# One ring of six PSUM banks for score tiles and all other products of three attentions

## The reference

```
xn = layernorm(x)
s  = attention_L(xn)          # L = 0, 1, 3: causal softmax attention; L = 2: linear attention over 64 x 64 maps
g  = silu(ffn_L(xn))          # L = 0, 3: mixture of 8 experts; L = 1: 8 experts and a shared one; L = 2: dense
x  = x + s * g
```

```
logits = q @ k^T (scaled), positions after the query masked
w      = softmax(logits)
out    = concat_heads(w @ v) @ Wo
```

## Time and profile before

| | us |
|---|---|
| median of 3 runs | 1986.79 |
| lowest, highest | 1980.47, 1986.86 |
| span of the profiled execution | 1987.3 |
| TensorE busy | 1839.8 (93%) |
| VectorE busy | 1337.9 (67%) |
| GpSimd busy | 1239.5 (62%) |
| ScalarE busy | 963.6 (48%) |

### The profile page before, as it was taken

How to read it: one execution, slowest core, us unless ns; L and a number is a source line. 1 busy time by engine, 2 the same in 40 slices (tenths; PEclk the granted TensorE clock), 3 DMA queues, 4 the chain that set the end, 5 groups by cost and what they waited for, 6 DMA issues and landing times.

```text
span 1987.3 us, 31683 instructions
## 1 busy us (share of the span) xinstructions
PE 1839.8 (93%) x9960; PEld 1273.0 (64%) x9960; DVE 1337.9 (67%) x3765; ACT 963.6 (48%) x2008; POOL 1239.5 (62%) x1454
## 2 busy tenths in 40 slices
PE   5999999999895899999999999999889999998985
PEld 4566666666595566676766567887556666555564
DVE  8888888888344767666666546556776777764533
ACT  2534445445455455554555534545344545444543
POOL 1767789889654467767777710011367888799953
PEclk8999999999998899999999999999799999999997
DMA  5224243232153443443444220000313223223243
GB/s 150 67 61 116 64 107 91 63 78 61 53 175 85 95 95 82 109 95 90 102 93 100 66 88 22 1 13 1 85 44 71 63 69 77 69 67 86 63 122 101
DMA packets 138508, 155.95 MB, mean 78 GB/s; under 512 B 34420, under 2 KB 78740, under 8 KB 138084
## 3 DMA queue, kind: packets, MB, share of 16 engines
q1 hardware_dynamic: 134244, 145.80, 30.0%
q0 software_dynamic: 4096, 8.12, 1.2%
HBM read 47.96 MB, written 17.52 MB: 33 GB/s over the span
## 4 chain that ended last, share of the span: by engine, by line
PE 62%; DVE 12%; POOL 11%; issue 6%; DMA 3%; ACT 3%; SPq 2%; POOLq 0%; DVEq 0%; ACTq 0%
PE P L904 61%; POOL acc L1701 4%; POOL yd L1724 3%; DVE mx L2112 2%; DMA qA<-hq 2%; POOL acc L1698 1%; SPq L1828 1%; DVE P L2123 1%; POOL xg L1715 1%; POOL pr L1679 1%; PE P L1003 1%; ACT pr L1444 1%; PE P L942 0%; DMA xl<-yd 0%; POOL z L1707 0%
## 5 line engine op out<-in xcount | busy, mean ns | idle before, releaser
L1701 POOL TENSOR_TENSOR acc<-acc,pr 128x512 f32<-128x512 f32 (+5 forms) x640 | 660.3, 1051 | 47.2 <-ACT pr L1444 22.5
L1444 ACT ACTIVATE pr<-P 128x512 f32<-128x512 f32 (+1 forms) x768 | 396.7, 568 | 321.4 <-PE P L904 278.8
L904 PE MATMUL P<-pr,vt 128*64 128x512 f32 (+3 forms) x2304 | 402.7, 490 | 4.9 <-POOL pr L1679 4.9
L904 PE MATMUL P<-qA,kA 128*128 128x512 f32 (+2 forms) x1024 | 389.2, 383 | 12.5 <-ACT pr L1444 11.6
L904 PE MATMUL P<-qB,kB 128*128 128x512 f32 (+2 forms) x1024 | 367.7, 365 | 0.0
L904 PE MATMUL P<-kA,qA 128*128 128x512 f32 (+2 forms) x1152 | 314.8, 376 | 32.0 <-DMA qA<-hq 12.3
L1679 POOL TENSOR_SCALAR_AFFINE_SELECT pr<-pr 128x256 f32<-128x256 f32 x384 | 157.3, 411 | 275.6 <-ACT pr L1444 214.6
L904 PEld LDWEIGHTS P<-pr,vt 128*64 128x64 f32 x2304 | 154.0, 137 | 225.7 <-issue 191.1
L2112 DVE TENSOR_REDUCE mx<-P 128x1 f32<-128x512 f32 x384 | 243.4, 683 | 40.2 <-PE P L904 37.9
L904 PEld LDWEIGHTS P<-qA,kA 128*128 128x128 f32 x1024 | 195.1, 191 | 95.7 <-ACT pr L1444 46.6
L904 PEld LDWEIGHTS P<-kA,qA 128*128 128x128 f32 x1152 | 194.5, 197 | 94.7 <-issue 25.0
(11 more groups left out here) (355 smaller groups left out, 2847.4 us busy)
## 6 DMA issues: line engine op xcount, KB each, us to landing
qA<-hq SPq DMA_DIRECT2D x384, 128.0 KB
kA<-stage SPq DMA_DIRECT2D x158, 128.0 KB
qB<-qB SPq DMA_DIRECT2D x96, 128.0 KB, 2.3
kB<-stage SPq DMA_DIRECT2D x79, 128.0 KB
rb<-sum_share SPq DMA_DIRECT2D x60, 128.0 KB
yd<-in_c_zero SPq DMA_DIRECT2D x32, 128.0 KB, 2.7
w<-in_L_W SPq DMA_DIRECT2D x16, 256.0 KB
xg<-xg SPq DMA_DIRECT2D x24, 129.0 KB
```

The costliest lines, as they stand in the source:

```text
L904: return P.matmul(out, lhs, rhs, start=start, stop=stop)
L1444: S.activation(a.pr[slot][:, r, 512 - wide:512], m.bank[b][:, 512 - wide:512], AF.Exp, scale=0.125).then_inc(s.free[b], 1)
L1701: G.tensor_tensor(acc[:, :, sl], acc[:, :, sl], pt[:, :, sl], ALU.add).then_inc(s.acc, 1)
```

## The change

The scores' own ring is gone. Score tiles take their banks from aux, which now has six banks in the order 4, 5, 6, 2, 0, 1. In layer 3's table one step, k0', moves behind q0'; it is done once, in the eighth job, where the keys of the second block are projected. And the identity products before the last output are left out where they would write into the bank that the output product itself uses.

```diff
-         "score": ("score", 2), "pv0": ("pv", 1), "close": ("aux", 1), "out": ("aux", 1), "nbias": ("aux", 1),
+         "score": ("aux", 2), "pv0": ("pv", 1), "close": ("aux", 1), "out": ("aux", 1), "nbias": ("aux", 1),
...
-POOLS = {"aux": (4, 5, 6, 2), "score": (0, 1), "pv": (3, 7), "misc": (3, 7), "up": (0, 1, 2, 3), "dn": (4, 5), "tr": (6, 7),
+POOLS = {"aux": (4, 5, 6, 2, 0, 1), "pv": (3, 7), "misc": (3, 7), "up": (0, 1, 2, 3), "dn": (4, 5), "tr": (6, 7),
...
-    3: ("q0 + k0' + k0 k1 q0' k0\" S V3 + R1 S q0\" + v0 C1 S S + M1 M0 F1 k1' S q1' q1 S + + W1 Z1 q1\" M2 I1 + "
+    3: ("q0 + + k0 k1 q0' k0' k0\" S V3 + R1 S q0\" + v0 C1 S S + M1 M0 F1 k1' S q1' q1 S + + W1 Z1 q1\" M2 I1 + "
...
-                    if pair == p and k[1:] == (1, 7, 1):
+                    if pair == p and k[1:] == (1, 7, 1) and od.bank[IDLE_OUT[L][1]][0][0] != b:
                         idle(*IDLE_OUT[L])
```

## The result

The changed kernel takes 1988.32 us in the median of 20 runs (1981.33 to 1996.48), the one before 1985.40 in 20 runs beside them (1979.64 to 1990.63). The ratio of changed to before is 1.0021, 95% interval 1.0011 to 1.0031: 2 to 6 us slower, under the 0.5% named before the run. The forecast of 1991.3 us was 3 us too high, 1.4 us of it because it started from the median of three runs (1986.79). The +4.5 us of its sum stands against +4.1 us by the ratio and +2.9 by the medians.

A forecast was written before the change was run, and what follows sets the result against it. TensorE was taken to bound the attentions, GpSimd 1743 to 1905 us. Terms -1.0 + 6.3 - 2.1 + 1.0 + 0.7 + 0 - 0.4 = +4.5 us on 1987.3, less 0.5, gave 1991.3 us; range 1975 to 2003.

The forecast's parts named there:

- The first attention: 80 to 535 us: +6.3 us net; eleven query-bank waits (ten at M2, one at a score) +7.1, maxima's banks +2.9, gains -3.7.
- The 14 scores behind a maximum's reader: First attention: 14 score tiles take a bank a maximum just used, mean 0.2 us each, together 2.9 us lost.
- The start: 0 to 80 us: key projection starts 2.0 us sooner in a free bank; 1.0 us taken as gained.
- The second attention: Net -2.1 us: 1.6 lost at 14 scores behind maxima; first maxima 1.0, last job's tiles and small waits 2.7 gained.
- Before the third attention: First key projection waits for L2493 to free the last gated product's bank: +1.0 us; then +0.7 up to 1743 us.
- GpSimd's stretch: 1743 to 1905 us: TensorE gets 1.6 us back, but GpSimd is full, so 0 on the path.
- R2: Rival, slower: GpSimd runs dry from 1743 us, idle above 15 us; 2002.2 or 1999 us; 0.21 with other such losses.
- The end: Last output product: nine warming matmuls fall away, 0.4 us gained.
- The upper bound of +1.1 us: Last output product: if TensorE's clock falls to 1.2 GHz after the rest, its 1.06 us doubles.
- R1: Rival, faster: more banks lift the score waits wholesale, 23 us less 7.1, giving 1971 us; chance 0.13.
- R3: Rival, no effect: the query bank is free in time, 7.1 us falls away, 1984 us; chance 0.20 shared with R4.
- R4: Rival: the ring is wider but each wait only changes its name, 1987 us; chance 0.20 shared with R3.

The follow-up runs named there:

- e1: Ring of six in layer 0 alone, layers 1 and 3 as in the kernel before: 1990.44 us against 1986.13 for the kernel before, ratio 1.0021.
- e4: Kernel before with its two rings, but layer 0's maximum M2 takes the query bank let go last: 1989.69 us against 1986.13, ratio 1.0016.
- e3: Changed kernel, but a held bank goes to the ring's end when let go: 1980.53 us against 1986.13 for the kernel before, ratio 0.9961.
- e2: Ring of six in layers 1 and 3 alone, layer 0 as in the kernel before: 1986.51 us, ratio 0.9990 to the kernel before.

## Why the prediction was right

**The first attention, +6.3 us forecast.** Right in place and sign. The mechanism was there as told: M2 right behind L2084, 0.67 us late at 367 us. But it wasn't the same in every job. Taking the excess over 0.23 us at M2 for the maxima of the third to the sixteenth job (85.77 to 486.07 us), the changed trace has 0.67 or 0.68 eight times, 0.58 and 0.59 once each, 0.16 once and nothing three times: ten jobs with a full wait, as counted, and 6.7 us in all, close to the 7.1. The waits between 170 and 505 us, changed kernel:

```profile
PE P L904 <- DVE qB L2084: 4.3, 9, 0.5
...
PEld P L904 <- DVE mx L2123: 3.8, 14, 0.4
...
PEld P L904 <- DVE qB L2084: 0.9, 1, 0.9
```

The one load wait of 0.9 us is the score that meets a query's bank (at 184.59), the forecast's eleventh place.

The 14 scores behind a maximum's reader are there too, 14 times as counted, with a mean of 3.8 / 14 = 0.27 us at the load. At the place of the earlier trace rows, 281.82 us in the changed kernel, the load waits 0.23 us for L2123, where the forecast had 0.29. So the two losses stand nearly as counted. The eleven jobs show +3.74 us, but they are 326 of the forecast's 455 us. From 58.67 to 118.03 us (57.64 to 118.87 in the changed kernel, M2 of the first and of the third job) it is +1.87, and from 118 to 177 us the two traces can't be compared, since the clock fell in one. The last job is a gain of 2.3 us (below), so that up to its output product some 3.4 us are seen, without that stretch, of the 6.3: the last job gives most of what is missing. By the ratio of e1 the layer costs 4.2 us (1.2 to 7.3), start and end included. That the query's bank is the cause of the loss in the eleven jobs and not merely beside it, e4 and e3 show: put alone into the kernel before it costs 4.7 us of those jobs, taken out of the changed one it gives 5.0.

That the 14 waits behind maxima cost 2.9 us, as the term has it, wasn't tested alone. In e3 they all stand, and the eleven jobs are 1.2 us shorter than before: 43 lifted score waits outweigh them, by that much. At 0.10 us each, the 43 are worth 4.3 us, so the 14 and all else cost about 3.1 us. This is worked out, not shown.

**The last job, which had no term of its own.** In the last job of the first attention no maxima stand between the score tiles. There a score that waits for its predecessor's reader is late in full. Kernel before, then changed kernel:

```profile
515.79 0.50 PE L904 MATMUL P<-qA,kA 128*128 128x512 f32 x1 [0.29 <-ACT pr L1444]
...
536.56 0.69 DVE L2185 TENSOR_TENSOR z<-P,rd 128x512 f32<-128x512 f32 x1
...
537.40 1.06 PE L904 MATMUL P<-wo,z 128*128 128x128 f32 x8
```

```profile
514.23 0.39 PE L904 MATMUL P<-qA,kA 128*128 128x512 f32 x1
...
534.54 0.69 DVE L2185 TENSOR_TENSOR z<-P,rd 128x512 f32<-128x512 f32 x1
534.56 3.36 PE L904 MATMUL P<-ident 128*128 128x128 f32 x14 [0.80 <-DVE rd L2179]
...
537.71 1.27 PE L904 MATMUL P<-wo,z 128*128 128x128 f32 x8
```

Tile follows tile every 1.50 us before (514.29 to 515.79), every 0.91 to 0.92 now (513.32 to 514.23). From the job's first score (503.97; 504.21) to the output product at 533.70 (531.68) the changed kernel is 2.26 us shorter. Then it loses this again. The identity products write into bank 0, in the kernel before long free by then. In the merged ring the last closing sum stands in it, and they wait for L2179, which reads it, and run at half the clock (0.50 from 532 to 538 us); the last output product comes 2.48 us after z is ready (535.23), before 0.15 (537.25). To the next stage (539.30; 539.82) the job is 0.28 us longer than before. In all six kernels with the ring of six in layer 0 and without the rule this figure is 2.48, with the two rings 0.05 to 0.15, with the rule 0.05 to 0.95. The forecast had these products stay as they are, at no cost; no experiment moved them alone.

**The start, -1.0 us.** As forecast. From the first projection of the first query to the first score the kernel before takes 29.51 us and the changed one 28.57, 0.94 less. The key projection gains 2.26 us; VectorE takes back the rest, since the product behind it waits for L2084 instead (23.80).

**The second attention, -2.1 us.** Too favourable. From the third to the sixteenth job the two traces differ by 0.33 us (393.54 before, 393.21 after), and from there to the next stage by 0.17 us (1124.78 to 1157.50; 1122.26 to 1154.81). At the place of the earlier trace rows in the changed kernel the score behind a maximum loses less than the 0.11 us forecast:

```profile
960.42 0.40 PE L904 MATMUL P<-qA,kA 128*128 128x384 f32 x1
...
960.66 0.34 PE L904 MATMUL P<-qB,kB 128*128 128x384 f32 x1
```

The two matmuls are 0.24 us apart instead of 0.18, 0.06 us. Load waits for L2112 went from 4 to 17 there (640 to 1160 us), 13 more where 14 were forecast, so the loss has its place and is smaller than the forecast's 1.6 us. So the gains, 3.7 us in the forecast, are the step that failed. The tiles of the last job did gain: at its last wide tile (1139.35; 1133.52) the changed kernel is 3.31 us further ahead than at the job's start. But the products of the values behind them then wait for GpSimd's mask (L1679, 0.2 us of open waits before, 2.4 now), and at the output product (1148.67; 1145.15) 1.0 us of it is left. The identity products take that: they wait 1.73 us for L2179, and the last output product comes 1.00 us after z, before 0.05. e2's 0.9990 lets -2 us stand as possible, the traces don't favour it.

**Before the third attention, +1.0 us.** As forecast, changed kernel:

```profile
1388.15 0.69 DVE L2493 TENSOR_TENSOR xf<-P,s 128x512 f32<-128x512 f32 x1 [8.80 <-PE P L904]
...
1388.95 0.19 PEld L904 LDWEIGHTS P<-xh,weights 128*64 128x64 f32 x2 [1.03 <-issue]
1388.98 0.65 PE L904 MATMUL P<-xh,weights 128*64 128x512 f32 x2 [0.87 <-DVE xf L2493]
```

The projection starts 0.14 us after L2493 ends; before, it started 0.28 us before L2493 began. From there to 1743 us the forecast was +0.7. From the third to the eleventh job it is 235.56 us before (from 1487.25) and 235.71 after, +0.15; from there to the sixteenth 158.61 and 159.66, +1.05. This last one lies where the clock of the changed kernel fell, and that of the kernel before did not:

```profile
1716.00:1719.40 3.40, 3.40 (x12) 2.03 (x12) 2.58 (x11) 0.93 (x3) 2.11 (x3) 0.53 0.02 6
```

Half the clock over 3.4 us is enough for it. So these traces don't show the +0.7.

**GpSimd's stretch, 0.** GpSimd's idle time is 162 - 152.59 = 9.4 us, as before, far from the 15 us at which R2 would have held. R2 didn't happen.

**The end, -0.4 us.** For the piece that the forecast names, as forecast. Changed kernel:

```profile
1907.25 5.50 PE L904 MATMUL P<-wo,z 128*128 128x128 f32 x32
...
1910.85 0.69 DVE L2185 TENSOR_TENSOR z<-P,rd 128x512 f32<-128x512 f32 x1
...
1913.59 0.94 PE L904 MATMUL P<-ident 128*128 128x128 f32 x6 [0.83 <-DVEq L1996]
```

z is ready at 1911.54 and the next stage starts at 1913.59, 2.05 us later; before, 1915.65 and 1918.08, 2.43. That is 0.38 us. The upper bound of +1.1 us asked for a fallen clock at this product; the stretches (columns as in the earlier trace rows) show it fallen before, behind a stretch in which TensorE was half idle, and full again when the product runs. In the kernel before it is 1.00 from 1897 to 1918 us. Changed kernel:

```profile
1897.00:1904.00 7.00, 3.52 (x18) 0.82 (x14) 0.00 (x0) 0.03 (x1) 6.75 (x7) 0.96 0.00 0
1904.00:1911.00 7.00, 6.35 (x28) 4.34 (x29) 2.24 (x4) 1.23 (x2) 1.21 (x3) 0.55 0.00 0
1911.00:1918.00 7.00, 5.73 (x40) 4.78 (x40) 2.92 (x5) 3.05 (x5) 0.00 (x0) 1.00 0.39 106
```

So the fallen clock that the bound spoke of did come, at the products ahead. Over the whole end, from the last products of the values (1909.54; 1904.54) to the next stage, the changed kernel takes 9.05 us and the one before 8.54: 0.5 us lost where 0.4 was to be gained.

**The rivals.** R1 (faster, the waits lifted wholesale) fails twice: the score waits did all go, and the kernel is slower. Nor did TensorE's open waits fall by 10 us: those for L1444, L2084, L2112, L2123 and L1679 come to 38.3 us before (11.6 + 4.3 + 10.0 + 7.5 + 4.9) and to 41.4 after (0 + 11.0 + 15.2 + 4.8 + 10.4). The Trainium skill ("Perfetto Trace Analysis", "Optimization Strategy") says that the same gap repeating on the engine that should be saturated can mean that there isn't enough PSUM for the next tile. Here the gap went with the ring of six, and the changed kernel is 0.2% slower; only with the bank order of e3 is it faster, by 0.4%. R3 (the query's bank is free in time) is excluded by the nine open waits for L2084 and by e4. R4 (each wait changes its name at no cost) holds for layers 1 and 3 as far as the runs resolve, not for layer 0.

**The sum.** The cause that the forecast names is there, with its size in each job. That the total came out so near is luck in part. In the first attention the last job gained 2.3 us more than was seen coming, and the identity products, which had no term, took it back; as far as the two traces can be compared, the second attention's -2.1 us was some 1.6 us too favourable and the end's -0.4 some 0.9.

## What to carry to other kernels

Merging two rings of banks doesn't only add room: each product then waits for another earlier reader. Walk the take order and set each reader's end against the new taker's start; a list ordered by take isn't ordered by when banks come free, and here a bank held for a late reader belonged at the end when it was let go. Walk the small products too that share a bank with the ring, like the identity products here. Here the merge alone cost 0.2%, and the merge with that rule gained 0.4%. Compare stretches of equal work at the same clock, not the spans of two profiles.

## What the hardware showed that was not expected

- A wait at the weight load is not a wait of its matmul. A load 0.27 us late left its own matmul in time and cost 0.10 us at the next; 43 such waits in the eleven jobs, 9.8 us at the loads, would be worth 4.3 us at that price. Where tile follows tile with nothing between, as in the last job, the same wait cost 0.58 us a tile (1.50 against 0.92 us).
- The time from the end of the releasing instruction to the matmul isn't one number. Where the load waited for the same release, both start 0.06 us behind it (23.74 to 23.80). Where the trace has no such wait at the load, the load starts 0.11 us and the matmul 0.14 us behind it (366.81 to 366.92 and 366.95; 1388.84 to 1388.95 and 1388.98). The forecast had 0.05 for all.
- TensorE's clock fell in different places from kernel to kernel, also where little or nothing differs between them: from 133 to 140 us it is 0.53 before, 1.00 after and, in e3, 0.76. The changed kernel's profiled span came out 4.3 us shorter while its runs are 4.1 us longer, so shifts of this size in one profile say nothing of a change.
